# Slot tables of their own for the first, middle and last image and the tail, and another order of the opening, in an attention kernel

## The chip, the cores and the metric

One core of a Trainium2 chip runs the whole program. The metric is the device time of one execution in microseconds (us). The engines are TensorE (PE, with its weight loads as PEld), VectorE (DVE), ScalarE (ACT), GpSimd (POOL) and the DMA queues that SyncE (SP), POOL and ACT issue on.

## The reference

Eight images of 256 channels and 1024 positions go through three blocks, all in 32-bit floats.

```python
# block 0: group norm, 8-head attention (head width 32), projection, residual
qkv = einsum('oc,bcl->bol', w_qkv, group_norm(x)) + b_qkv
weight = softmax(einsum('bct,bcs->bts', q * scale, k * scale), axis=1)   # over the queries' axis
x = x + einsum('oc,bcl->bol', w_proj, einsum('bts,bcs->bct', weight, v)) + b_proj
t = to_tokens(x)
# block 1: layer norm, linear attention with elu(.)+1 features and rope, plus a 3-tap convolution
q, k = elu(ln(t) @ Wqk + bqk) + 1
t = t + rope(q) @ (rope(k)^T @ v) / (q . mean(k)) + conv3(ln(t))
# block 2: layer norm, Haar transform, interpolation, fc1, gelu, fc2, inverse Haar
t = t + idwt(fc2(gelu(fc1(interp(ll)))), lh, hl, hh)
```

## The kernel before

**Units.** The attention of an image is cut into 64 units: two groups of four heads, eight blocks of 128 keys, four heads. A unit s is: `scores` on PE (one 128x1024 product in the two-bank buffer `ps_s[s % 2]`), `maximum` on DVE (`negmax`, line 937), `exponentials` on ACT (`probs`, line 805). After each four units DVE inverts the sums (line 943, `rsums`), POOL scales the values by them (line 1213, `v_scaled`) and PE multiplies them with the probabilities (`weigh_values`, `ps_o`, line 585). q and k are each split in a high and a low part (`high_part` on ACT, line 839, `low_part` on DVE, line 982), and small DMAs stack these on the partitions of `q_st` and `k_st`: 16 of 128 KB for q and twice 16 of 64 KB for k, for each group of heads.

**Slots.** Each engine runs an in-order program, written out at build time: for each s from 0 to 63 first the unit's own instruction, then the steps that a hand-written table gives to slot s. PE runs one unit ahead: in slot s it issues `scores(s + 1)` first and then the steps. The steps are the rest of the work: `..._POST` tables hold blocks 1 and 2 of the image before (proj, x1T, lnT, qk, kT, kv, den, denT, out, uT, rT, ll, fc1, fc2, on POOL rsqrt, lepe, turn, pairs), `..._NEAR` tables the projections of this image's second group, `..._AHEAD` tables the next image's load, group norm (stats, moments, gn, squares, affine, apply) and first projections (pq0, pk0, pv0). Between engines only semaphores count, so that a slot number is an order on one engine and no moment. The same tables serve every image; the inverting, scaling and `weigh_values` stand in the loops at fixed places (s % 4 equal to 0, 1 and 2), as do the evictions of `ps_o` (slots 3, 4, 35, 36).

**Banks.** All steps of PE share two PSUM banks, `work[0]` and `work[1]`. `banks()` hands them out in turn over one middle image, and the prologue, the first and the last image take the same numbers, also where steps are missing and two tiles in a row get one bank. `claim` makes PE wait until the reader of the bank's tile before has read it. After the last image (`epilogue`) the tail's tables run with six banks.

**Opening.** SP loads the first image in two halves, then small constants, parameters and `w_qkv` (one semaphore, `early_in`), then the rest. PE waits for `early_in`, runs `warm_up(8)` (16 small products), the group means, `warm_up(18)`, then the tiles in the order pq0, pq0, pv0, pk0, pk0, pv0, and `scores(0, 0)`. SP stacks q of heads 0 and 1 and then k pieces, POOL q of heads 2 and 3 and then k pieces, ACT the k pieces of head 2.

## Time and profile before

| | us |
|---|---|
| median of 3 runs | 1459.22 |
| lowest and highest run | 1455.28, 1461.02 |
| the profiled execution | 1459.43 |
| its span, first to last instruction | 1457.6 |
| mean granted clock of TensorE | 0.944 |
| busy in the span: PE, DVE, ACT, POOL | 1228.9, 993.8, 878.9, 468.6 |

The page's fifth part groups the instructions by line; its second part cuts the span in 40 slices. The opening goes to about 38.6 us (the first `maximum`), each of the six middle images takes about 167 us, and the tail begins at 1352.4 us. Within a middle image a stretch is named by its times in image 2, which runs from 353.8 to 521.7 us.

### The profile page before, as it was taken

To read this page: it belongs to the slowest core of one execution; us is meant where nothing else is said; L and a number is where in the kernel's file an instruction comes from. 1 tells how busy PE (TensorE), PEld (TensorE's weight loads), DVE (VectorE), ACT (ScalarE), POOL (GpSimd) and SP (SyncE) were. 2 spreads that over 40 slices of the span, in tenths; PEclk is the share of its full clock that TensorE was granted. 3 is DMA by queue.
4 is the path that set the end of the run, shared out by engine and by line. 5 is a ranking of instruction groups with operands and counts; after the bars stand their busy time and mean duration, and the time that the engine had idled before them with its cause. 6 is when DMAs were issued, how large, how long until landed. Compare 5 with 4: busy or idle time off the path is not lost.

```text
span 1457.6 us, 21670 instructions
## 1 busy us (share of the span) xinstructions
PE 1228.9 (84%) x7724; PEld 621.8 (43%) x7724; DVE 993.8 (68%) x1607; ACT 878.9 (60%) x1457; POOL 468.6 (32%) x623
## 2 busy tenths in 40 slices
PE   5777799788987898889997899888988899979856
PEld 4423344444444444444444444444544444434343
DVE  2566587856878487766877568794878668784561
ACT  1556567665775667665774657656676657756412
POOL 2001016520364006530164203650065302650360
PEclk9798899999999999999999999999999999999977
DMA  7142315333242233432242232522243333310111
GB/s 250 31 117 62 80 32 106 71 85 98 62 108 60 55 83 86 89 87 78 66 80 78 63 99 61 114 55 56 81 92 84 87 81 71 76 50 15 35 24 44
DMA packets 51355, 111.27 MB, mean 76 GB/s; under 512 B 15505, under 2 KB 15761, under 8 KB 50993
## 3 DMA queue, kind: packets, MB, share of 16 engines
q1 hardware_dynamic: 48576, 100.85, 28.6%
q0 software_dynamic: 2480, 8.78, 2.0%
q8 instruction: 62, 1.02, 0.3%
q14 instruction: 45, 0.36, 0.1%
q10 hardware_dynamic: 192, 0.26, 0.1%
HBM read 21.75 MB, written 8.39 MB: 21 GB/s over the span
## 4 chain that ended last, share of the span: by engine, by line
PE 49%; DVE 24%; ACT 8%; issue 6%; SPq 5%; DMA 4%; POOL 2%; DVEq 0%; ACTq 0%; POOLq 0%
DVE negmax L937 11%; PE ps_s L570 11%; PE ps_o L585 11%; ACT probs L805 5%; PE work L716 4%; PE work L597 4%; PE work L721 4%; PE work L658 4%; PE work L644 4%; SPq L417 3%; PE work L609 3%; DVE ln_st L1002 3%; DVE tok L1013 3%; DMA xg<-in_x 2%; DVE t L1087 1%
## 5 line engine op out<-in xcount | busy, mean ns | idle before, releaser
L937 DVE TENSOR_REDUCE negmax<-ps_s 128x1 f32<-128x1024 f32 x512 | 619.7, 1214 | 294.1 <-PE ps_s L570 292.4
L805 ACT ACTIVATE probs<-ps_s,negmax 128x1024 f32<-128x1024 f32 x512 | 570.3, 1114 | 375.4 <-DVE negmax L937 369.9
L570 PE MATMUL ps_s<-q_st,k_st 128*128 128x512 f32 x1024 | 418.1, 494 | 118.0 <-ACT probs L805 106.5
L570 PEld LDWEIGHTS ps_s<-q_st,k_st 128*128 128x128 f32 x1024 | 171.0, 197 | 368.8 <-ACT probs L805 226.1
L585 PE MATMUL ps_o<-probs,v_scaled 128*32 128x512 f32 x2048 | 264.5, 637 | 5.1 <-POOL v_scaled L1213 5.1
L1213 POOL TENSOR_TENSOR v_scaled<-v_tok,rsums 128x128 f32<-128x128 f32 x128 | 51.3, 401 | 613.9 <-DVE rsums L943 613.9
L597 PE MATMUL work<-xg,w_qkv 128*128 128x512 f32 x256 | 122.9, 604 | 1.5 <-DVE t L1087 1.5
L585 PEld LDWEIGHTS ps_o<-probs,v_scaled 128*32 128x32 f32 x2048 | 56.1, 115 | 143.8 <-issue 131.4
L658 PE MATMUL work<-ln_ch,w_qk 128*128 128x512 f32 x232 | 110.6, 599 | 8.0 <-DVE k_ch L1113 8.0
L1272 POOL TENSOR_TENSOR x<-x,csum 128x1024 f32<-128x1024 f32 x45 | 106.7, 2370 | 3.2
L805 ACT ACTIVATION_READ_ACCUMULATOR probs<-ps_s,negmax 128x1 f32 x512 | 99.6, 195 | 0.0
L609 PE MATMUL work<-w_qkv,xg 128*128 128x128 f32 x512 | 67.8, 293 | 8.5 <-DVE lo L982 8.5
L839 ACT ACTIVATE hi<-work,par 128x512 fp32r<-128x512 f32 x62 | 42.3, 683 | 53.2 <-PE work L597 48.8
L716 PE MATMUL work<-band,w 128*128 128x512 f32 x118 | 63.6, 669 | 12.2 <-ACT band L877 12.2
L609 PEld LDWEIGHTS work<-w_qkv,xg 128*128 128x128 f32 x512 | 66.0, 207 | 14.1 <-DVE lo L982 12.0
L1244 POOL TENSOR_TENSOR ln_var<-ln_mv,con 128x2 f32<-128x2 f32 x64 | 13.1, 205 | 170.0 <-DVE ln_mv L1007 170.0
L597 PEld LDWEIGHTS work<-xg,w_qkv 128*128 128x128 f32 x256 | 47.1, 190 | 47.6 <-issue 35.0
L982 DVE SCALAR_TENSOR_TENSOR lo<-work,par,hi 128x512 fp32r<-128x512 f32 x62 | 46.4, 748 | 28.6 <-ACT hi L839 27.4
L658 PEld LDWEIGHTS work<-ln_ch,w_qk 128*128 128x128 f32 x232 | 42.7, 190 | 45.3 <-issue 28.6
L721 PE MATMUL work<-shared,w 128*128 128x512 f32 x128 | 60.3, 597 | 0.9 <-ACT shared L880 0.9
L644 PE MATMUL work<-att,w_proj 128*128 128x512 f32 x120 | 56.8, 597 | 0.0
L869 ACT ACTIVATE t<-work,par_elu 128x512 f32<-128x512 f32 x58 | 39.6, 683 | 26.0 <-PE work L658 26.0
(143 smaller groups left out, 1383.2 us busy)
## 6 DMA issues: line engine op xcount, KB each, us to landing
q_st<-hi SPq DMA_DIRECT2D x124, 128.0 KB, 2.4
q_st<-lo SPq DMA_DIRECT2D x124, 128.0 KB, 2.4
k_st<-hi SPq DMA_DIRECT2D x240, 64.0 KB, 2.0
k_st<-lo SPq DMA_DIRECT2D x240, 64.0 KB, 2.0
x<-in_x SPq DMA_DIRECT2D x8, 1024.0 KB, 5.0
out_x<-ln_ch SPq DMA_DIRECT2D x16, 512.0 KB, 2.8
xg<-in_x POOLq DMA_DIRECT2D x7, 1024.0 KB, 7.1
t<-shared SPq DMA_DIRECT2D x64, 64.0 KB, 2.3
```

The lines of the kernel that those rows point to most:

```text
L570: mm = pe.matmul(ps_s[s % 2][:, half * HALF:half * HALF + HALF], k_st[:, h, j * P:j * P + P], q_st[g][:, h, half * HALF:half * HALF + HALF ...
L585: mm = pe.matmul(ps_o[D * h:D * h + D, cols], v_scaled[:, j % 2, D * h:D * h + D], probs[:, j % 2, h, cols], start=(j == 0), stop=(j == NB ...
L597: mm = pe.matmul(bank(tile)[:, :], w_qkv[:, c, col:col + P], xg[:, c, half * HALF:half * HALF + HALF], start=(c == 0), stop=(c == NC - 1))
L609: mm = pe.matmul(bank(tile)[:, P * n:P * n + P], xg[:, c, P * nb:P * nb + P], w_qkv[:, c, col:col + P], start=(c == 0), stop=(c == NC - 1))
L644: mm = pe.matmul(ps[:, :], w_proj[:, g, P * c:P * c + P], att[:, g, half * HALF:half * HALF + HALF], start=(g == 0), stop=(g == 1))
L658: mm = pe.matmul(ps[:, :], w_qk[:, c, col:col + P], ln_ch[:, c, 1 + half * HALF:1 + half * HALF + HALF], start=(c == 0), stop=(c == NC - 1))
L716: pe.matmul(ps[:, :], w1[:, P * n:P * n + P], band[:, :], start=True, stop=True)\
L721: mm = pe.matmul(ps[:, :], w2[:, k, :], hid[:, k, :], start=(k == 0), stop=(k == 7))
L805: act.activation(probs[:, j % 2, h, :], ps_s[s % 2][:, :], ACT.Exp, bias=negmax[:, s % 4:s % 4 + 1], accum_out=sums[:, j % 2, h:h + 1]).th ...
L937: dve.tensor_reduce(negmax[:, s % 4:s % 4 + 1], ps_s[s % 2][:, :], AX_X, ALU.max, negate=True)\
L1213: pool.tensor_tensor(v_scaled[:, j % 2, :].rearrange("p (h d) -> p h d", h=HG), v_tok[g][:, j, :].rearrange("p (h d) -> p h d", h=HG), r.t ...
L1272: pool.tensor_tensor(x1[:, c, :], x1[:, c, :], lepe_product, ALU.add).then_inc(lepe_step, 1)
```

## The change

The shared tables go. Each engine gets a table for the first image, the middle ones, the last and the tail; the inverting ("invert"), scaling ("scale"), `weigh_values` ("values"), the evictions of `ps_o` ("copy") and the folding of a weight ("w1") are entries in them, at the slots that they had. Banks are handed out in turn over the whole program, image by image. Many steps stand in other slots. Of the tail's tables nearly all numbers are new; its order changes in places (kT tiles behind qk.6 and qk.7, uT.0 ahead of kv.1, `ll` ahead of the rT tiles). In the opening the constants and parameters are issued ahead of the image and have a semaphore of their own, k's first tile is made first, k of heads 0 to 2 is stacked first and then q head by head, rows 0 and 1 by SP and rows 2 and 3 by POOL; `warm_up(18)` becomes `warm_up(20)`, and PE waits for the scaled weights only behind it.

The middle images, slots of the steps that move (before, after):

```
PE    x1T.2 9,10  qk.6 27,28  den 32,31  denT 36,32  out.0 36,35  out.2 39,40  uT.0 40,39  uT.1 41,39
      uT.2 42,41  gn 38,39  rT.1 51,50  rT.3 52,51  fc1.1 49,48  pv0.1 60,56
ACT   x1T.1 9,10  x1T.2 10,11  qk.0 17,18  qk.3 23,22  qk.6 27,28  den 34,31  rT.3 52,51  ll 49,48
      apply.0 40,41  pq0 44 45,43 44
DVE   norm1.1 12,14  norm2.0 43,42  norm2.2 45,46  proj.2 8,9  x1T.2 11,12  qk.0 19,18  qk.1 20,19
      qk.3 24,23  qk.5 26,27  qk.6 28,29  kv.0 29,30  denT 36,33  out 38 38 40 42,37 39 41 41
      uT 41 42 43 43,40 40 42 43  up.0 63,61  stats 34 34 35 36,28 33 34 37  moments 37,38  gn 39,40
      pq0.0 45,44  pv0.1 61,63
POOL  rsqrt1 11 12 13 14,12 12 13 15  rsqrt2.0 38,39  kmean 29,32
      lepe 15 16 17 20 20 21 22 23 25 25 26 28,15 19 21 21 21 23 24 24 24 25 25 26
      turn 28 30 35 36 36 37,28 32 34 35 36 36  pairs.0 44,43  load 29,23  squares 37,38  affine 37,42
```

The core of the rest of the diff:

```diff
+FIRST_TILES = [("gn", 0), ("pk0", 0), ("pq0", 0), ("pq0", 1), ("pk0", 1), ("pv0", 0), ("pv0", 1)]
...
             def prologue():
+                for dst, src in ((con[:, 0:EARLY], consts[:, 0:EARLY]), (par[:, :], params)):
+                    sp.dma_start(dst, src).then_inc(const_in, DMA)
                 for c in range(NC):
                     sp.dma_start(xg[:, c, :], x_v[0][:, c]).then_inc(x_first[c], DMA)
-                for dst, src in ((con[:, 0:EARLY], consts[:, 0:EARLY]), (par[:, :], params),
-                                 (w_qkv[:, :, :], wqkv_t)):
-                    sp.dma_start(dst, src).then_inc(early_in, DMA)
+                sp.dma_start(w_qkv[:, :, :], wqkv_t).then_inc(early_in, DMA)
...
+                stack_first_k(sp, [(h, row) for h in range(3) for row in (0, 1)], first_stacked)
                 stack_first_q(sp, (0, 1), first_stacked)
-                stack_first_k(sp, ((0, 0), (0, 1), (1, 0), (1, 1), (3, 0), (3, 1)), first_stacked)
                 stack_k(sp, 0, 0, 1)
...
-        def stack_first_q(eng, heads, signals):
-            eng.wait_ge(lo_done, 2)
+        def stack_first_q(eng, rows, signals):
+            eng.wait_ge(lo_done, 1 + nth_split(0, ("pq0", 1)))
...
-                pe.wait_ge(early_in, EARLY_LOADS)
+                pe.wait_ge(const_in, CONST_LOADS)
                 warm_up(8)
-                pe.wait_ge(weights_ready, 1)
-                for tile in claimed(PE_AHEAD):
+                for tile in FIRST_TILES:
                     pre_tile("prologue", -1, tile)
                     if tile[0] == "gn":
-                        warm_up(18)
+                        warm_up(20)
+                        pe.wait_ge(weights_ready, 1)
                 scores(0, 0)
...
+                    for tile in due("PE", kind, s):
+                        step(kind, i, tile)
-                    if kind == "first":
-                        for tile in due(s, FOLD_AT):
-                            fold(kind, i, tile)
-                    if post:
-                        post_slot(kind, i, s)
-                    for tile in due(s, PE_NEAR, PE_AHEAD if ahead else {}):
-                        pre_tile(kind, i, tile)
-                    if s % HG == PV_AT:
...
-                stack_first_k(act, [(2, row) for row in range(4)], first_stacked)
+                stack_first_k(act, [(3, row) for row in range(4)], [first_stacked_act] * HG)
...
+                stack_first_k(pool, [(h, row) for h in range(3) for row in (2, 3)], first_stacked_pool)
                 stack_first_q(pool, (2, 3), first_stacked_pool)
-                stack_first_k(pool, ((0, 2), (0, 3), (1, 2), (1, 3), (3, 2), (3, 3)), first_stacked_pool)
```

## Rows read from the trace of the kernel before

**Rows 1.** The head of the page: the span.
```profile
span 1457.6 us, 21670 instructions
```

**Rows 2.** Windows by stage: length, busy us (instructions) per engine, clock, DMA share, GB/s.
```profile
core 0: us, PE busy (x) PEld busy (x) DVE busy (x) ACT busy (x) POOL busy (x), PEclk, DMA share, GB/s
38.60:185.20 146.60, 115.11 (x474) 48.16 (x473) 89.68 (x102) 84.29 (x140) 9.06 (x25) 0.83 0.29 72
...
353.80:521.70 167.90, 147.47 (x962) 75.07 (x961) 122.51 (x201) 109.47 (x182) 59.25 (x77) 0.98 0.33 79
...
688.80:863.30 174.50, 152.01 (x961) 76.20 (x960) 122.90 (x201) 109.47 (x182) 59.17 (x77) 0.95 0.32 76
...
1197.50:1352.40 154.90, 133.53 (x891) 65.42 (x894) 112.84 (x183) 102.74 (x173) 56.19 (x67) 0.96 0.24 58
1352.40:1457.60 105.20, 70.59 (x509) 41.67 (x508) 47.09 (x110) 29.75 (x46) 38.07 (x39) 0.79 0.14 36
```

**Rows 3.** Timeline of the opening to 18 us: start, length, engine, line, tiles, [idle before].
```profile
4.64 2.59 DVE L952 BATCH_NORM_STATS2 gn_stats<-xg 128x6 f32<-128x512 f32 x4 [4.64 <-DMA xg<-in_x]
...
9.39 0.50 DVE L1169 TENSOR_SCALAR w_qkv<-w_qkv 128x256 f32<-128x256 f32 x2 [1.83 <-DMA w_qkv<-in_wqkv_t]
...
9.41 3.78 PE L748 MATMUL ps_s<-con 128*128 128x128 f32 x16 [9.41 <-DMA w_qkv<-in_wqkv_t]
...
13.27 4.47 PE L748 MATMUL ps_s<-con 128*128 128x128 f32 x36
13.45 0.16 DVE L966 COPY gn_grp<-work 128x4 f32<-128x4 f32 x1 [3.34 <-PE work L615]
...
16.15 1.24 ACT L818 ACTIVATE xg<-xg,gn_sh,gn_a 128x1024 f32<-128x1024 f32 x1 [6.55 <-POOL gn_sh L1221]
...
17.57 3.60 PE L597 MATMUL work<-xg,w_qkv 128*128 128x512 f32 x8
```

**Rows 4.** Timeline of the opening from 21 to 45 us.
```profile
21.93 0.75 DVE L982 SCALAR_TENSOR_TENSOR lo<-work,par,hi 128x512 fp32r<-128x512 f32 x1 [0.96 <-ACT hi L839]
...
27.27 0.75 DVE L982 SCALAR_TENSOR_TENSOR att<-work,par,att 128x512 fp32r<-128x512 f32 x1 [0.96 <-ACT att L839]
...
30.80 4.89 SPq L433 DMA_DIRECT2D k_st<-att  x6
...
37.37 2.08 PE L570 MATMUL ps_s<-q_st,k_st 128*128 128x512 f32 x4 [8.96 <-DMA k_st<-att]
...
43.58 1.17 PE L570 MATMUL ps_s<-q_st,k_st 128*128 128x512 f32 x4
```

**Rows 5.** Windows: the stretch in which the first stacking lands.
```profile
27.00:38.00 11.00, 2.04 (x15) 1.75 (x14) 1.44 (x2) 0.23 (x1) 3.06 (x7) 0.67 0.91 233
```

**Rows 6.** Windows: two stretches of image 2.
```profile
432.40:475.70 43.30, 33.64 (x315) 20.10 (x312) 37.09 (x75) 24.42 (x40) 24.46 (x34) 0.96 0.33 91
480.00:506.00 26.00, 26.00 (x98) 11.20 (x96) 11.47 (x12) 15.85 (x26) 0.80 (x2) 1.00 0.02 3
```

**Rows 7.** Timeline of DVE, 432 to 476 us, image 2.
```profile
437.90 1.29 DVE L952 BATCH_NORM_STATS2 gn_stats<-xg 128x6 f32<-128x512 f32 x2 [1.87 <-DMA xg<-in_x]
...
453.16 0.68 DVE L1087 TENSOR_TENSOR t<-work,t 128x512 f32<-128x512 f32 x1
...
454.83 1.19 DVE L937 TENSOR_REDUCE negmax<-ps_s 128x1 f32<-128x1024 f32 x1
...
472.00 1.23 DVE L937 TENSOR_REDUCE negmax<-ps_s 128x1 f32<-128x1024 f32 x1 [2.05 <-PE ps_s L570]
```

**Rows 8.** Timeline of PE, 432 to 480 us, image 2.
```profile
441.67 0.73 PE L570 MATMUL ps_s<-q_st,k_st 128*128 128x512 f32 x2 [2.16 <-ACT probs L805]
...
467.97 3.53 PE L609 MATMUL work<-w_qkv,xg 128*128 128x128 f32 x16 [1.41 <-DVE lo L982]
```

**Rows 9.** Timeline of all engines, 500 to 522 us, the end of image 2.
```profile
506.84 0.75 DVE L982 SCALAR_TENSOR_TENSOR lo<-work,par,hi 128x512 fp32r<-128x512 f32 x1 [1.75 <-ACT hi L839]
...
520.38 1.19 PE L570 MATMUL ps_s<-q_st,k_st 128*128 128x512 f32 x4 [0.30 <-DMA k_st<-lo]
```

**Rows 10.** Timeline of image 2 near slot 19.
```profile
396.36 1.92 PE L585 MATMUL ps_o<-probs,v_scaled 128*32 128x512 f32 x16 [0.58 <-POOL v_scaled L1213]
```

More of the change, by code:

```diff
@@ L91 @@
[L91 to L97 removed]
+PE_FIRST = {
+    "w1": (25, 27), "pq1": (11, 12), "pv1": (0, 0), "pk1": (19, 20), "gn": (39,), "pq0": (43, 44),
+    "pk0": (49, 56), "pv0": (45, 56), "values": (6, 10, 14, 18, 22, 26, 30, 34, 38, 42, 46, 50, 54, 58, 62),
+}
@@ L546, in claim @@
             def claim(kind, i, tile):
-                before, earlier = tile_before(kind, tile)
+                before, earlier = tile_before(i, tile)
                 if before is None:
```

437 lines of the change are left out of this document (226 added, 211 removed), and 23 rows, old and new, of tables (DVE_LAST, DVE_POST, DVE_STEADY, DVE_TAIL).

## The prediction

> **What bounds the kernel now.** I read the windows by stage first, then the timelines of the stretches in which an engine idles. Rows 2 split the span: the first image takes 146.6 us, a middle one 167.9 us with PE busy for 147.5 and DVE for 122.5, the last 154.9, the tail 105.2. So 20.4 us in a middle image are not PE work: that is all that an order of steps can give there, if PE keeps its work. No single engine is the bound throughout. Three kinds of stretch are to be seen in image 2. From 480 to 506 us PE is busy for 26.00 of 26.00 us [rows 6]: it is the bound. From 432.4 to 475.7 us PE is busy for 33.6 of 43.3 us but DVE for 37.1 [rows 6]: DVE is the bound, and where it idles the time is lost: 1.87 us for the next image's load, 2.05 us for a score [rows 7]. From 507.6 us, where the low part of the last k tile ends (506.84 + 0.75), to 520.38 us the chain is 16 small DMAs and their landing, and the next image's first score waits 0.30 us for them [rows 9]: this chain of 12.8 us hangs from the low part alone. The opening is a fourth kind: until 37.37 us no score runs, and PE stands idle for 8.96 us before it, waiting for stacked k [rows 4].
>
> Image 4 (688.8 to 863.3) is 6.6 us longer than image 2 with the same instructions [rows 2]. It belongs to this execution; I leave it in the sum and give it as a spread.
>
> **The opening, first half.** Before, PE begins to warm up at 9.41, when `w_qkv` is there; the group means follow its 16 products, and the copy of them is at 13.45, though the statistics had ended at 7.23 [rows 3]. After, constants and parameters are issued first, so PE warms up while the image lands. The image is issued two transfers later. The gap between two issues of SP stands in no row here; from the second load on the bytes ahead are the same, so I take the statistics 0 to 1.3 us later (the upper end is half their own 2.59), 1.0 taken. They end at 8.2, and with means and squares the product of the means is at 9.2. DVE still has to scale the weights behind `w_qkv` (9.39 + 0.50 [rows 3], and three small ones): the copy is at 10.1. From the copy to the apply it took 16.15 - 13.45 = 2.70, and the apply 1.24 [rows 3]: the normed image is there at 14.0, where it was at 17.4.
>
> But `warm_up(20)` is 40 products, begun at 9.5 us. The first 16 took 3.78 us, 0.236 each, the 36 behind them 4.47 us, 0.124 each [rows 3]: the two levels of the clock. At the fast one they end at 14.5, at the slow one at 18.9. PE's first warming products lie before a hole of about 1 us, so neither is excluded. I take the fast level from the first quarter on: PE's first projection at S = 15.5, before at 17.57 [rows 3]. The gain is 2.1, bounds -1.3 and 3.1.
>
> The Trainium skill ("TensorE: Matmul & The Clock Gate", Part 1) says that the fast clock is the answer to activity and goes with idleness, and that its windows run free of the program. By that rule the split warming could go the slow way in one execution and the fast way in the next. It is the third rival.
>
> **The opening, second half.** Before, the low part of q was there at 22.68 and that of k at 28.02; SP issued q of heads 0 and 1 first and its last six k pieces at 30.80 to 35.69; heads 0 and 1 both began at 37.37, heads 2 and 3 at 43.58, behind PE's pv1 tiles [rows 4]. That is 19.8 and 26.0 us behind the first projection. The stacking itself is bound by transfer: from 27 to 38 us the DMA engines are busy for 0.91 and move 233 GB/s [rows 5]. Its 16 x 128 KB and 16 x 64 KB are 3.1 MB, 13.5 us at that rate. After, nothing of this volume goes away; what changes is when it starts and what a head waits for. k's first tile is ready 3.5 us behind S (a tile of four products is 3.60 / 2 = 1.8 [rows 3]; high part, low part and their waits, 1.7, a little above twice 0.75). Twelve k pieces then take 0.8 MB, 3.4 us at the rate of rows 5, about 2.5 us to landing. q's second tile comes 1.8 us behind q's first; its low part is there at S + 6.8. A head's q is 0.5 MB, 2.3 us. So head 0 is complete at about S + 11, head 1 at S + 13, head 2 at S + 15.5, head 3 at S + 18. PE has its seven tiles done at S + 11 too. Then score 0, score 1, and the two pv1 tiles (43.58 - 39.4 = 4.2, [rows 4]) until S + 18, scores 2 and 3 at S + 18 to S + 19.5, that is 33.5 to 35, where they were at 43.58. The gain behind score 3 is 8.5 to 10, the whole opening 10.0 with the first half's part in it; bounds 6 and 12.
>
> **The first image.** Its order hardly changes; the banks now alternate, the statistics move into slots where DVE idles in any case (busy for 89.7 of 146.6 [rows 2]). 0, with 2.5 either way for the clock, which is 0.83 there [rows 2] and follows PE's gaps.
>
> **Middle images, to slot 31.** POOL's convolution steps (lepe) gave way late to a scaling, and PE waited 0.58 us for `v_scaled` [rows 10]. The new table has one step between those two scalings and seven between the next two, with the load behind them. That block is long, but the next values on PE are two slots off. I take 0.3 (PE loses part again where qk.6 goes one slot back), bounds -0.7 and 1.0.
>
> **Middle images, slots 32 to 48.** This is the term that counts. The load leaves POOL's order at 23 rather than 29, so some 20 us earlier than the statistics need it: DVE's 1.87 and, in the units' ring, PE's 2.16 [rows 7, 8] go (one event, counted once). One statistic (1.29 / 2 = 0.65 [rows 7]) leaves the stretch. denT is made early and fills PE's time. The pv0 tile took 3.53 us for 16 products behind a gap of 1.41 [rows 8], at a clock of which rows 6 show 0.96 for the whole stretch; DVE's 2.05 is that tile's shadow [rows 7]. Against it stands a new wait: `gn` on PE (slot 39) now takes uT.0's bank, so PE waits there for DVE's slot 40, and `scores(41)` is queued behind it; DVE then does two uT tiles of 454.83 - 453.16 = 1.67 us each [rows 7] before it copies `gn`. The ceiling is DVE's own work: 43.3 - 37.1 + 0.65 = 6.9 us. The floor is 0: every idle moment replaced by another. I take 1.87 + 2.05 gone, a quarter of the remaining 2.3 of idleness gone, 1.0 given to the new wait: 3.5.
>
> **Middle images, slots 49 to 63.** PE is the bound to 506 us [rows 6] and its work is the same, so the 3.5 pass through. pv0.1 moves from slot 60 into PE's wait in slot 57; that gives nothing, since the chain of 12.8 us [rows 9] sets the end. So a middle image gives 3.8; six of them 22.8.
>
> **Last image and tail.** The last image has no load, statistics or gn; 1.0, bounds 0 and 3. The tail's order moves a few waits; POOL's turning steps stay one chain. 0, 3 either way.
>
> **Sum.** 10.0 + 22.8 + 1.0 = 33.8 from the profiled execution's 1459.4 (its span is 1457.6 [rows 1]), which is the median of the runs to 0.2 us: 1426.
>
> **The rivals.** (1) Waits replaced. DVE and PE only trade waits in slots 32 to 48, and a middle image gives 1.0: 1459.4 - 9 - 6 = 1444. For it: ACT, DVE and PE wait for each other in a ring of two score buffers, so that a gap closed at one place opens at the next. Against it: the 1.87 us are a wait for a transfer, which no reordering of the ring brings back. 0.25. (2) All idleness of DVE in the stretch goes but a fifth: 5.5 + 0.3 per image, 12 in the opening: 1459.4 - 34.8 - 12 - 1 = 1412. For it: DVE has no gap but these in rows 6. 0.12. (3) The clock is slow in `warm_up(20)`: S = 18.9 rather than 15.5, all else as forecast: 1429. 0.13. (4) Slower. The new claim of `gn`: its copy comes behind two uT tiles, then POOL's affine chain (behind rsqrt2.1) and the apply on ACT, in front of the exponentials and of pq0, whose low part starts everything up to the next image. By my order pq0 still begins about 1 us earlier than before. It decides from the point where the copy comes over 1 us later than that; at two uT tiles more, 3.3 us, each image loses 2.3 beyond what it gained: 1459.4 - 10 + 13.8 = 1463. 0.04. (5) The tables change but the engines' order in time doesn't, since slots are no moments; the opening alone acts: 1449. 0.06. The forecast has 0.40.
>
> **How the numbers follow.** 1426 is the likeliest case's. Its own terms reach from 1418 to 1436. The range 1411 to 1446 takes in rivals 1, 2 and 3 and leaves out 4 and 5, some 2 in 10 with the edges; the 6.6 us of image 4, which may be there or not, are within it. About 0.5% (7.3 us) is what a measurement of this kernel can tell from no change, so faster begins below 1452: the forecast, 1, 2, 3 and nearly all of 5, less a little for unforeseen waits, 0.91. Same 0.05, slower 0.04.
>
> **What would show it.** In the changed kernel's profile: PE's first L597 near 15.5, the first score near 27 and scores 2 and 3 by 35, with heads one after the other; the copy of the means at 10. No idle time of DVE before L952 in any middle image. A middle image of about 164 us, with the stretch from slot 32 to 48 down to about 40 us, and PE still full from fc1 to fc2. It is wrong if PE shows gaps of over 1 us before L615 with a release by DVE t, if ACT's L818 starts later in the image than before, or if the middle images come out above 167.

## The result: 1397.1 us, nearly twice the forecast gain

The changed kernel takes 1397.1 us (median; 1393.4 to 1398.3), the kernel before on the same chip 1458.6; the ratio is 0.958 with a 95% interval of 0.955 to 0.960. The forecast was 1426 us, its range 1411 to 1446: 61.5 us were gained where 33.8 had been worked out. The profiled execution took 1396.6 us, so the trace stands for the median to 0.6 us. Three single runs of experiments that were far longer than the others of their kernel (1912.9, 6427.5 and 1647.0 us) are left out of the times below. Its span, from the head of its page:

```profile
span 1394.8 us, 21679 instructions
```

The windows by stage (columns as in [rows 2]; first image, image 2, last image):

```profile
30.60:175.70 145.10, 112.51 (x475) 48.35 (x476) 89.83 (x102) 84.51 (x140) 9.03 (x25) 0.85 0.33 81
336.30:496.10 159.80, 146.27 (x959) 73.78 (x959) 122.33 (x200) 109.34 (x182) 59.09 (x77) 0.99 0.35 83
...
1138.00:1289.10 151.10, 135.80 (x893) 66.24 (x896) 113.52 (x184) 103.11 (x173) 56.16 (x67) 0.96 0.24 56
```

Against [rows 2], PE's busy time in image 2 is nearly the same (146.3 for 147.5), the image is 8.1 us shorter, and 13.5 us are left in which PE is idle, of 20.4. Cut at the first `maximum` of each image (slots by the order of the 512 `maximum` instructions), the two traces differ like this, in us:

| | before | after | gain | forecast |
|---|---|---|---|---|
| start of image 1 (opening and first image) | 185.2 | 175.7 | 9.5 | 10.0 |
| six middle images, slots 0 to 31, mean of one | 77.5 | 75.0 | 2.5 | 0.3 |
| slots 32 to 48 | 45.0 | 40.5 | 4.5 | 3.5 |
| slots 49 to 63 | 46.2 | 44.9 | 1.3 | 0 |
| last image | 155.0 | 151.2 | 3.8 | 1.0 |
| tail | 105.2 | 105.8 | -0.6 | 0 |

Opening and slots 32 to 48 came out near the forecast. The excess lies in slots 0 to 31, in slots 49 to 63 and in the last image, 24 us together; slots 32 to 48 add 1.0 in each of six images.

The first line stands for one execution. The changed kernel and the thirteen variants below that keep its opening have the same first image, and it ends between 175.1 and 181.4 us in their traces (mean 177.7); with the opening of before it ends between 185.2 and 186.0. So 8 us is the better figure for this line, and 175.7 is one of the luckier executions.

In the changed kernel's code the lines are others: `scores` is L608 (was 570), `weigh_values` L623 (585), `maximum` L970 (937), `exponentials` L841 (805), the projections L635 and L647 (597, 609), qk on PE L696 (658), kT L704, its DVE part L1146 (1113), gn L653, out L736, ll L749, fc1 L754, the copy of ll's band on ACT L913 (877), the turning steps on POOL L474 to L480.

The opening in the timeline of the changed kernel (PE's two warm-ups, copy of the means, first projection, the four first scores):

```profile
3.45 3.78 PE L794 MATMUL ps_s<-con 128*128 128x128 f32 x16 [3.45 <-DMA par<-in_params]
...
9.78 6.34 PE L794 MATMUL ps_s<-con 128*128 128x128 f32 x40
9.96 0.16 DVE L999 COPY gn_grp<-work 128x4 f32<-128x4 f32 x1
...
15.96 7.21 PE L635 MATMUL work<-xg,w_qkv 128*128 128x512 f32 x16
...
29.78 0.73 PE L608 MATMUL ps_s<-q_st,k_st 128*128 128x512 f32 x2 [2.93 <-DMA q_st<-hi]
33.83 1.22 PE L608 MATMUL ps_s<-q_st,k_st 128*128 128x512 f32 x2 [3.31 <-DMA q_st<-hi]
34.85 5.41 PE L647 MATMUL work<-w_qkv,xg 128*128 128x128 f32 x32
40.02 1.17 PE L608 MATMUL ps_s<-q_st,k_st 128*128 128x512 f32 x4
```

It answers to [rows 3, 4]: the means are copied at 9.96 (forecast 10.1), the first projection starts at 15.96 (15.5), the first score at 29.78 (27), scores 2 and 3 at 40.02 (33.5 to 35).

### The profile page after: what moved, and what is told of

It reads as the page before. It is cut to its first block, busy times and chain, and to the rows that moved or that the text cites. A ratio compares the mean times of both kernels' runs of the same rounds, so it can differ in the third digit from the quotient of the medians.

```text
span 1394.8 us, 21679 instructions
## 1 busy us (share of the span) xinstructions
PE 1227.2 (88%) x7728; PEld 621.5 (45%) x7728; DVE 992.1 (71%) x1607; ACT 879.8 (63%) x1457; POOL 467.0 (33%) x623
## 4 chain that ended last, share of the span: by engine, by line
PE 53%; DVE 28%; ACT 9%; issue 6%; SPq 1%; DMA 1%; POOL 0%; DVEq 0%; POOLq 0%; ACTq 0%
DVE negmax L970 13%; PE ps_s L608 12%; PE ps_o L623 12%; ACT probs L841 7%; PE work L696 6%; PE work L635 4%; PE work L759 4%; PE work L754 3%; DVE tok L1046 3%; PE work L682 3%; DVE ln_st L1035 3%; PE work L647 2%; PE work L736 2%; DVE t L1120 1%; DVE lo L1015 1%
## 5 line engine op out<-in xcount | busy, mean ns | idle before, releaser
L970 DVE TENSOR_REDUCE negmax<-ps_s 128x1 f32<-128x1024 f32 x512 | 620.0, 1215 | 243.2 <-PE ps_s L608 241.6
L841 ACT ACTIVATE probs<-ps_s,negmax 128x1024 f32<-128x1024 f32 x512 | 570.4, 1114 | 321.4 <-DVE negmax L970 316.3
L608 PE MATMUL ps_s<-q_st,k_st 128*128 128x512 f32 x1024 | 408.7, 485 | 78.0 <-ACT probs L841 67.9
L608 PEld LDWEIGHTS ps_s<-q_st,k_st 128*128 128x128 f32 x1024 | 168.8, 195 | 328.3 <-ACT probs L841 198.1
L623 PE MATMUL ps_o<-probs,v_scaled 128*32 128x512 f32 x2048 | 267.6, 643 | 0.5 <-POOL v_scaled L1240 0.5
L635 PE MATMUL work<-xg,w_qkv 128*128 128x512 f32 x256 | 122.2, 601 | 2.8 <-ACT xg L854 2.8
L623 PEld LDWEIGHTS ps_o<-probs,v_scaled 128*32 128x32 f32 x2048 | 55.9, 113 | 133.7 <-issue 132.1
L696 PE MATMUL work<-ln_ch,w_qk 128*128 128x512 f32 x236 | 113.0, 601 | 2.4 <-DVE k_ch L1146 2.3
L841 ACT ACTIVATION_READ_ACCUMULATOR probs<-ps_s,negmax 128x1 f32 x512 | 99.5, 194 | 0.0
L635 PEld LDWEIGHTS work<-xg,w_qkv 128*128 128x128 f32 x256 | 47.9, 191 | 49.4 <-issue 39.8
L754 PE MATMUL work<-band,w 128*128 128x512 f32 x118 | 57.1, 615 | 10.0 <-ACT band L913 5.9
L647 PEld LDWEIGHTS work<-w_qkv,xg 128*128 128x128 f32 x512 | 62.5, 196 | 5.5 <-issue 3.3
L647 PE MATMUL work<-w_qkv,xg 128*128 128x128 f32 x512 | 62.6, 280 | 0.0
L1015 DVE SCALAR_TENSOR_TENSOR lo<-work,par,hi 128x512 fp32r<-128x512 f32 x62 | 46.2, 745 | 22.6 <-ACT hi L875 22.6
L696 PEld LDWEIGHTS work<-ln_ch,w_qk 128*128 128x128 f32 x236 | 43.1, 190 | 40.6 <-issue 29.1
L1296 POOL TENSOR_SCALAR csum<-ln_ch,par 128x1024 f32<-128x1024 f32 x45 | 54.0, 1199 | 0.0
```

What stands on the lines that cost most here:

```text
L608: mm = pe.matmul(ps_s[s % 2][:, half * HALF:half * HALF + HALF], k_st[:, h, j * P:j * P + P], q_st[g][:, h, half * HALF:half * HALF + HALF ...
L623: mm = pe.matmul(ps_o[D * h:D * h + D, cols], v_scaled[:, j % 2, D * h:D * h + D], probs[:, j % 2, h, cols], start=(j == 0), stop=(j == NB ...
L635: mm = pe.matmul(bank(tile)[:, :], w_qkv[:, c, col:col + P], xg[:, c, half * HALF:half * HALF + HALF], start=(c == 0), stop=(c == NC - 1))
L647: mm = pe.matmul(bank(tile)[:, P * n:P * n + P], xg[:, c, P * nb:P * nb + P], w_qkv[:, c, col:col + P], start=(c == 0), stop=(c == NC - 1))
L696: mm = pe.matmul(ps[:, :], w_qk[:, c, col:col + P], ln_ch[:, c, 1 + half * HALF:1 + half * HALF + HALF], start=(c == 0), stop=(c == NC - 1))
L754: pe.matmul(ps[:, :], w1[:, P * n:P * n + P], band[:, :], start=True, stop=True)\
```

## The experiments

Unless it is said otherwise, an experiment is the changed kernel with one part put back or moved; two are the kernel before with one part of the change. The step tables are meant; what isn't named stays. "More" and "less" compare with the 1397.1 us above. The changed kernel was timed only then; the kernel before came out at 1457.0 to 1460.3 us in the rounds of the experiments, and one variant, timed in two rounds, at 1400.3 and 1406.4. So a difference of under some 6 us between two kernels below is not firm.

### One part put back at a time

**The opening** of before (order of the loads, starts, warm-ups, tile order, stacking).

> The changed kernel (1397.1 us) with the opening of before: image issued ahead of the constants, PE, ACT and POOL waiting for the weights too, 18 warming calls, tiles in the order q, q, v, k, k, v, q of heads 0 and 1 stacked by SP and of heads 2 and 3 by POOL ahead of the k pieces. All slot tables stay new. Theory A (the opening's gain is what the fourth maximum shows, 45.5 us before and 41.9 us after): about 3.6 us slower, 1400.7, and the first image's new table keeps the other 5.9 us that the start of image 1 has gained (185.2 to 175.7). Theory B (as forecast, the opening is worth 10 and the first table nothing): 1407.

Measured 1405.6 (1403.7 to 1409.1), 8.5 more, near what theory B had. The first score is at 37.43, and image 1 starts at 185.7 us, as in the kernel before (185.2): the first image's new table gives nothing by itself.

**Load and statistics.**

```diff
-"load": (23,)                +"load": (29,)
-"stats": (28, 33, 34, 37)    +"stats": (34, 34, 35, 36)
```

> The changed kernel with POOL's load of the next image back at slot 29 and DVE's four statistics back at slots 34, 34, 35, 36. Theory A (the wait for the load cost every middle image its own length, as forecast): DVE idles 1.6 to 2.5 us in front of the statistics again and six images lose 2 to 2.7 us each, 12 to 16 us in all: 1409 to 1413. Theory B (with the other slots redrawn there is room for the wait, or the wait was shadowed by PE): under 4 us, below 1401.

Measured 1410.6 (1408.0 to 1412.4), 13.5 more, as theory A had it; by which mechanism is told below, and it isn't the one expected.

**qk and kv.**

```diff
 PE  -"qk": (17, 18, 21, 22, 24, 25, 28, 29)  +(17, 18, 21, 22, 24, 25, 27, 29)
 ACT -"qk": (18, 18, 21, 22, 24, 25, 28, 30)  +(17, 18, 21, 23, 24, 25, 27, 30)
 DVE -"qk": (18, 19, 22, 23, 25, 27, 29, 31)  +(19, 20, 22, 24, 25, 26, 28, 31)
 DVE -"kv": (30, 35)                          +(29, 35)
```

> The changed kernel with the steps of qk (PE, ACT, DVE) and DVE's kv back in their old slots, 17 to 31, middle images and last. Theory A (a q or k tile read one slot sooner frees its bank before PE gets there, which the forecast had not counted): 2 to 3 us for each of seven images, 1411 to 1418, with PE's gap of about 1.1 us at the fifth qk tile back. Theory B (as forecast, 0.3 us per image): 1397 to 1399.

Measured 1413.0 (1412.2 to 1414.7), 15.9 more: the largest part, where the forecast had 1.8.

**Slots 31 to 47** (den, denT, out, uT, norm2, gn, moments, turn, pairs and what goes with them).

> The changed kernel with den, denT, out, uT, norm2, moments, gn, squares, affine, apply, pq0's eviction, kmean, turn, rsqrt2 and pairs back in their old slots (31 to 47); load and statistics stay early. Theory A (the redrawn order there is worth about 2 us per image beside the load): seven images, 12 to 16 us slower, 1409 to 1413. Theory B (the early load does it all and the order itself gives nothing): within 3 us of 1397.

Measured 1409.5 (1403.8 to 1413.9), 12.4 more: theory A.

**POOL's lepe.**

> The kernel after with POOL's slots of the local term (lepe) as in the kernel before, in the steady and last tables, nothing else. The single parts so far undone sum to 50.4 of 61.5 us; the rest, 11, lies in the parts not yet undone and in the 7 us of image 4. Theory A (POOL's queue is a bound in slots 20 to 28: lepe ahead of the turning steps makes the kv products late): 6 x 1 us and more, 1403 or above. Theory B (lepe fills POOL's idle time and only its order changes): within 2 us of the changed kernel, 1395.5 to 1399.

Measured 1398.8 (1395.0 to 1400.8), 1.6 more, no difference that can be told: theory B.

**The late steps** (rT, fc1, ll, pv0.1, up).

> The kernel after with rT, fc1, ll, the second value tile pv0.1 and the upsampled rows (up) in the slots of before. In the median middle image, slots 49 to 63 are 1.0 us shorter after the change, mostly at slots 58 and 59. Theory A (pv0.1 in PE's wait for the DMA chain at slot 56 to 57 is what takes that 1.0 away, since PE doesn't fall to its slow clock before the products of the next image): 6 x 1.0 and 1 for rT, 1404 (1402 to 1406). Theory B (the chain of transfers sets the end, as the prediction had it, and pv0.1's place gives nothing): 1397 to 1399.

Measured 1406.3 (1401.3 to 1409.4), 9.2 more. By its size this spoke for theory A; the separation below shows that pv0.1 isn't the cause.

The six parts sum to 61.1 of 61.5 us. That they meet so well is in part luck: the 13.5 us of the load hold some 8 us of a collision that neither kernel has (below), so that without it the parts give 53, and 8 us of the gain are in none of them. The tail's tables and the new order of the banks were not put back by themselves. Whether the parts are independent was asked with **three put back together** (qk and kv, load, slots 31 to 47):

> The kernel after with three parts undone together that were undone singly before: the qk and kv slots, the early load with its statistics, and the order of slots 31 to 47. Singly they cost 15.9, 13.5 and 12.4 us, 41.8 together, against the changed kernel's 1397.1. Theory A (separate gaps on one bound chain, each worth its own time wherever it stands): the costs add, 1438.9 (1434 to 1443). Theory B (the three open the same slack: one new wait hides part of another, so that each single undo counts a shared loss twice, once it is there the next costs less): about 30 us, 1427. Theory C (they support each other, and what is left of the change doesn't work without them): beyond 46 us, over 1443.

Measured 1435.2 (1429.9 to 1436.7), 38.1 more against 41.8 by the sum, nearer to theory A. But in this kernel `kmean` stands ahead of the load again and the collision isn't there: POOL's turning step waits for no copy. Against the single costs without the collision, 34, the three together cost 4 more. Neither difference is beyond the spread, so the run speaks against theories B and C and says no more.

### The qk ring: eviction slots or PE's slots?

```diff
 ACT -"qk": (18, 18, 21, 22, 24, 25, 28, 30)  +(18, 18, 21, 23, 24, 25, 28, 30)
 DVE -"qk": (18, 19, 22, 23, 25, 27, 29, 31)  +(19, 20, 22, 24, 25, 26, 29, 30)
```

> The kernel after with the evictions of qk tiles 3 to 5 on ACT (slots 23, 24, 25 for 22, 24, 25) and on DVE (24, 25, 26 for 23, 25, 27, and tile 6 and 7 at 29, 30 for 29, 31) as in the kernel before, PE's slots as changed. The whole qk part cost 15.9 us, 2.5 in slots 24 to 31 of each middle image. Theory A (ring of two work buffers: PE waits for an eviction one slot late, ACT for PE, DVE for ACT; the evictions' slots alone make the gap): 6 x 1.5 to 2.5, 1406 to 1412. Theory B (PE's slots of the tiles decide): within 3 us of the kernel after, to 1400.

Measured 1421.5 (1420.7 to 1429.2), 24 more: theory A in kind, worse in size. DVE's eviction of tile 7 went to slot 30 here, where neither kernel has it (31 in both), and so ahead of DVE's copy of kv in the same slot; PE then waits for that copy, in image 2:

```profile
416.04 0.66 PE L704 MATMUL work<-con,k_ch 128*128 128x128 f32 x4 [2.37 <-DVE kv_c L1078]
```

So this kernel shows where the wait of the ring comes from, not what it costs. What evictions one slot late do is seen in the timelines (idle time before an instruction, and its releaser, in brackets). The kernel before, image 2:

```profile
409.90 1.23 DVE L937 TENSOR_REDUCE negmax<-ps_s 128x1 f32<-128x1024 f32 x1 [1.38 <-PE ps_s L570]
...
411.91 1.99 PE L658 MATMUL work<-ln_ch,w_qk 128*128 128x512 f32 x4 [1.14 <-DVE k_ch L1113]
...
413.99 0.69 ACT L869 ACTIVATE t<-work,par_elu 128x512 f32<-128x512 f32 x1 [1.57 <-PE work L658]
```

The changed kernel, the same slots:

```profile
391.73 1.23 DVE L970 TENSOR_REDUCE negmax<-ps_s 128x1 f32<-128x1024 f32 x1
...
392.51 1.88 PE L696 MATMUL work<-ln_ch,w_qk 128*128 128x512 f32 x4
...
394.48 0.69 ACT L905 ACTIVATE t<-work,par_elu 128x512 f32<-128x512 f32 x1 [0.23 <-PE work L696]
```

The kernel with the evictions alone put back:

```profile
395.37 1.22 DVE L970 TENSOR_REDUCE negmax<-ps_s 128x1 f32<-128x1024 f32 x1 [1.37 <-PE ps_s L608]
...
397.38 1.99 PE L696 MATMUL work<-ln_ch,w_qk 128*128 128x512 f32 x4 [1.14 <-DVE k_ch L1146]
```

DVE waits 1.38 for a score, PE 1.14 for DVE's reading of a qk tile, ACT 1.57 for PE: one loop, three waits. The slots of ACT and DVE make it: with PE's as changed and theirs back (ACT tile 3; DVE tiles 0, 1, 3 and 5), the same 1.37 and 1.14 return. Which of these tiles does it wasn't taken apart. The windows of slots 24 to 31 in image 3 say what it is worth. Before:

```profile
577.60:599.00 21.40, 19.08 (x210) 9.45 (x208) 17.01 (x29) 15.41 (x26) 11.18 (x13) 1.00 0.47 91
```

After, and behind it slots 32 to 39, 40 to 48 and 49 to 55:

```profile
551.50:570.90 19.40, 18.49 (x208) 9.07 (x206) 16.86 (x27) 14.35 (x26) 14.39 (x15) 1.00 0.66 150
...
570.90:587.00 16.10, 14.12 (x208) 7.61 (x207) 14.72 (x26) 10.96 (x19) 11.33 (x9) 1.00 0.24 55
...
587.00:611.80 24.80, 21.79 (x121) 13.31 (x119) 23.19 (x51) 13.77 (x22) 13.35 (x25) 0.93 0.31 83
611.80:636.10 24.30, 22.87 (x97) 10.58 (x97) 9.34 (x10) 19.89 (x31) 0.95 (x3) 1.00 0.21 47
```

PE is busy for 18.5 of 19.4 us there now: it had 2.3 idle, it has 0.9. Then the other way round, **qk and kv alone in the kernel before**, with nothing else changed:

> The kernel before, with the qk and kv slots of after on PE, ACT and DVE and nothing else. Taken out of the changed kernel they cost 15.9 us, 2 to 2.5 us in slots 24 to 31 of each image. Theory A (a wait in a ring of PE, ACT and DVE, removed by taking qk tile 3 out of the buffer a slot sooner; what stands elsewhere in the image plays no part): slots 24 to 31 fall from 21.35 to about 19.4, 1459 - 12 to 16: 1443 to 1447. Theory B (POOL's turning steps and kmean in their old slots take the place of the wait at once): under 6 us, 1453 or above.

Measured 1438.3 (1437.4 to 1440.4), 17 to 19 less than the kernel before in those rounds (ratio 0.988, interval 0.984 to 0.993). Its window of the same slots:

```profile
572.10:591.50 19.40, 18.64 (x209) 9.26 (x207) 16.26 (x26) 14.37 (x26) 11.15 (x13) 1.00 0.50 96
```

It is the changed kernel's 19.4 in the old surroundings: theory A, and more than it had. The ring itself gives 1.9 us in each of six middle images and the last, 13.6 us. The rest stands in slots 32 to 48 (45.0 before, 43.7 here), where the clock is slow in slots 40 to 48 of one middle image rather than four, and a stop of PE in image 4, told below, is 0.92 us rather than 4.19; that part may be this execution's. With qk put back in the changed kernel slots 24 to 31 take 21.9 us in all six images. So four lines of slot numbers are worth 14 to 16 us by themselves.

### The late steps: the value tile or the fold?

**rT, fc1 and ll put back**, pv0.1 as changed:

```diff
 PE  -"rT": (47, 50, 51, 51)  +(47, 51, 51, 52)
 PE  -"fc1": (48, 48, 49, 49, 49, 49, 49, 49)  +(48, 49, 49, 49, 49, 49, 49, 49)
 ACT -"rT": (47, 51, 51, 51), "ll": (48,)  +(47, 51, 51, 52), "ll": (49,)
```

> The kernel after with the slots of before for rT, fc1 and ll alone (pv0.1 and up as changed). All of the late part together cost 9.2 us; in its trace slots 49 to 55 were 26.36 us in most middle images against 24.34, with a gap of 2.04 us on PE ahead of fc1 (now 0.84 and 0.60), and slots 56 to 59 up to 13.5 against 11.89. Theory A (the wait before fc1 is the cause of the first: it is a loss of 0.6 by itself and drops the clock for the products behind it): most of the 9.2, 1404 to 1410. Theory B (pv0.1 out of slot 56 is the cause of both): 1396 to 1400.

Measured 1408.3 (1403.5 to 1413.7), 11.2 more. **pv0.1 and up put back**, the rest as changed:

> The kernel after with the slots of before for the second value tile (PE 60, DVE 61) and the upsampled rows (63, 63) alone, rT, fc1 and ll as changed. Theory A (the wait before fc1 makes the loss in slots 49 to 55): slots 49 to 55 stay at 24.3; slots 56 to 59 become 13 in some images, slots 60 to 63 become 7.95 rather than 8.69, and the first twelve 24.9 rather than 25.4: 1395 to 1400. Theory B (pv0.1 in slot 56 holds the clock and gives the 9.2): 1403 to 1408.

Measured 1395.2 (1390.5 to 1399.0), 1.9 less than the changed kernel, within the spread. Theory A both times: the fold carries all, the value tile nothing. Image 3 of the kernel with the fold put back, first ACT, then PE:

```profile
623.35 1.11 ACT L841 ACTIVATE probs<-ps_s,negmax 128x1024 f32<-128x1024 f32 x1
...
624.46 0.58 ACT L913 COPY band<-work 128x512 f32<-128x512 f32 x1
```

```profile
625.17 1.67 PE L754 MATMUL work<-band,w 128*128 128x512 f32 x2 [2.03 <-ACT band L913]
625.85 1.84 PE L608 MATMUL ps_s<-q_st,k_st 128*128 128x512 f32 x2
627.49 7.48 PE L754 MATMUL work<-band,w 128*128 128x512 f32 x14
```

The changed kernel, first ACT, then PE:

```profile
612.96 0.57 ACT L913 COPY band<-work 128x512 f32<-128x512 f32 x1
613.43 1.13 ACT L841 ACTIVATE probs<-ps_s,negmax 128x1024 f32<-128x1024 f32 x1
```

```profile
613.68 1.96 PE L754 MATMUL work<-band,w 128*128 128x512 f32 x4 [0.84 <-ACT band L913]
615.07 1.03 PE L608 MATMUL ps_s<-q_st,k_st 128*128 128x512 f32 x2
616.70 5.79 PE L754 MATMUL work<-band,w 128*128 128x512 f32 x12 [0.60 <-ACT shared L916]
```

With `ll` in ACT's slot 48 the copy goes ahead of an exponential of 1.1 us, and PE waits 0.84 and then 0.60 us rather than once 2.03. These 0.6 us are the smaller part. Behind the wait of 2.03 the next score takes 1.84 us rather than 1.03: the granted clock is 0.50 there, TensorE at 1.2 GHz and not at 2.4. Slots 49 to 55 take 26.6 us (mean of six), against 24.3. The windows of these slots and of the slow stretch in the same image (the changed kernel's, above, has 1.00):

```profile
622.10:648.40 26.30, 24.27 (x97) 11.22 (x97) 9.34 (x10) 19.95 (x31) 0.95 (x3) 0.94 0.19 43
...
625.60:629.00 3.40, 3.40 (x6) 1.68 (x5) 1.22 (x1) 1.42 (x2) 0.00 (x0) 0.50 0.52 117
```

The Trainium skill ("TensorE: Matmul & The Clock Gate", Part 1) says that activity releases the throttle and idleness brings it back. In direction these rows agree: in these slots the slow clock followed a wait of 2.03 us in all six images and one of 1.74 (before) in three. Behind one of 0.84 it is in none of the changed kernel's images, but in two with pv0.1 put back and in three with the load in slot 32 (slots 49 to 55 at 25.1 to 25.2 us). So a shorter wait makes it rarer and doesn't exclude it.

**The same three steps alone in the kernel before:**

> The kernel before, with three steps in the slots of after and nothing else: rT (slots 47, 50, 51, 51 on PE, 47, 51, 51, 51 on ACT), ll on ACT in 48, and the second tile of fc1 in slot 48 on PE. Taken out of the changed kernel they cost 11.2 us: PE then waits 2.03 us for ACT's band ahead of fc1, and the matmuls behind run at the slow clock. In the kernel before that wait is 1.74 us, and slots 49 to 55 take 24.7 us in three images and 26.3 in the others. Theory A (the wait and the clock behind it are a loss by themselves, whatever the other parts are): slots 49 to 55 become 24.3, 0.4 to 2 us per image, the median 1459 - 7 to 11: 1448 to 1452. Theory B (it gives only in the changed kernel's surroundings): 1456 to 1461.

Measured 1452.9 (1451.0 to 1458.2), ratio 0.997 (0.996 to 0.999): 4.3 us. The mechanism is the same (slots 49 to 55 fall from a mean of 25.5 to 24.6, PE's wait from 1.74 to 0.82 and 0.59), but less than theory A had: slots 56 to 59 rise from 12.8 to 13.1, they are long (13.0 to 13.5) in five of six images where they were in four. In the changed kernel they take 11.9 in all six; with pv0.1 put back, 12.8 in the mean. So pv0.1 in slot 56 does gain there, and gives it back in slots 60 to 63 (8.7 for 7.9) and 0 to 11.

### The load: traffic or collision?

In the kernel with the load in slot 29, POOL's and PE's timelines show in image 3:

```profile
572.72 0.79 POOL L424 DMA_DIRECT2D xg<-in_x  x1
...
581.21 2.00 POOL L474 TENSOR_TENSOR att<-att,con 128x1024 f32<-128x1024 f32 x1 [4.65 <-DMA att<-shared]
```

```profile
592.43 1.13 PE L736 MATMUL work<-kv_c,shared 128*128 128x128 f32 x8 [2.32 <-issue]
```

SP's last copy `att<-shared` was issued at the same moment as the load of 1 MB, and POOL's turning step waited for it 4.65 us, to 1.0 us behind the load's last packet (580.2). PE's wait is put down to "issue", but it ends where POOL's last turning step does (589.99 + 2.34 = 592.33). To separate this from traffic as such, a **spare transfer** of the same size in slot 29 for which nobody waits, with the load in 23:

> The kernel after, its load where it is (slot 23), and a second transfer of the same image (1 MB, same queue, from the input to a spare tensor in the chip's memory) issued by POOL in slot 29 of each middle image, for which nobody waits. With the load itself moved to slot 29 a kernel took 13.5 us more, and in its trace PE's long waits at L736 end with POOL's turning steps, which had waited for the copies att<-shared; DVE's wait for the load was not there. Theory A (it is the traffic of the load in slots 29 to 34 that makes the copies for the turning steps late): the spare transfer costs as much with nobody waiting for it, 1397 + 8 to 14, some 1408. Theory B (it is the statistics' place or DVE's wait for the load that costs, not the traffic): 1397 to 1400.

> The same kernel as in the run with the spare transfer in slot 29, again, because its profile of then can't be read (granted clock 0.582); 3.2 to 4.9 us more than the kernel after were measured. Theory A (collision with the copies att<-shared): POOL idle 2 us and more at L474 for the DMA att<-shared in some of the middle images, where the kernel after has none, and slots 32 to 39 longer in just these. Theory B (traffic plays no part): no such idle time, and slots 32 to 39 as in the kernel after, 15.8 to 16.1 us.

Measured 1400.3 in the first (1397.6 to 1403.8) and 1406.4 (1404.0 to 1414.0) in the second: 3 and 9 more, though nobody waits for it. The second's trace has what theory A asked for: POOL waits 1.9 to 5.1 us for `att<-shared` in five images, with slots 32 to 39 at 17.3 to 20.1 us, and not in the sixth, with 16.0. Last, the **load in slot 32**, behind the turning step that waits:

```diff
-"load": (23,)               +"load": (32,)
-"stats": (28, 33, 34, 37)   +"stats": (36, 36, 37, 37)
```

> The kernel after with the load in slot 32 of the middle images, in POOL's queue right behind the turning step that waits for the copies att<-shared, and the statistics in slots 36, 36, 37, 37. With the load in slot 29 (13.5 us more), SP's last of eight copies att<-shared was issued together with the load (572.77 and 572.72 in one image) and landed only 8 us later, for which POOL's turning step idled 4.65 us and behind it PE's tiles at L736. Here the load is issued later still, but with no copy of that kind under way. Theory A (the load costs by its collision with these copies alone): near the kernel after, 1397 to 1402. Theory B (a load of 1 MB in slots 29 to 36 costs wherever it is, by its traffic beside the k_st transfers or by the late statistics): 1407 to 1415.

Measured 1402.8 (1398.2 to 1404.5), 5.7 more, just beyond theory A's range. What ended the waits of POOL before its steps on `att`, summed over the span (us, times): load in 29, then the spare transfer:

```profile
  DMA att<-shared: 15.3, 5
```

```profile
  DMA att<-shared: 14.9, 5
```

In the kernel before, after, and with the load in 32 there is no such wait. In the last the order is:

```profile
575.21 2.00 POOL L474 TENSOR_TENSOR att<-att,con 128x1024 f32<-128x1024 f32 x1
577.15 0.79 POOL L424 DMA_DIRECT2D xg<-in_x  x1
```

So more than half of the 13.5 us is a collision that my experiment made: in the kernel before the load is in slot 29 too, but `kmean` stands ahead of it in POOL's queue and waits for k, so that the load is issued 4.8 to 6.7 us behind SP's last copy in the six middle images, and no turning step waits. In the changed order nothing holds it back, and it meets them. Putting one step back isn't the same as the step's share of the gain. What is left for a late load without the collision is 5.7, at the edge of what can be told, with slots 32 to 39 at 17.3 us rather than 15.9 (means of six). Some 15 us of POOL's waiting went with 13.5 and 9.3 us of time. The load alone moved to slot 23 in the kernel before wasn't run, so what the early load gives of the 61.5 us isn't shown.

### Three more

**gn ahead of uT** (PE 39 to 38, DVE 40 to 39): the forecast's rival 4 had seen a wait there.

> The kernel after with PE's product of the group means (gn) one slot earlier, ahead of the first two uT tiles, and its copy on DVE one slot earlier, as in the kernel before; nothing else. In the changed kernel PE waits 1.10 and 0.69 us there in a middle image, for DVE's uT additions. Theory A (those two waits are a loss that the place of gn makes): they go, and some 1 to 1.8 us per image with a gn come back, 1386 to 1391, faster than the kernel after. Theory B (the ring of buffers closes on PE in any case, and the means are then behind POOL's squares, which PE would wait for): no gain, 1396 to 1400; with the means late, slower, up to 1405.

Measured 1401.9 (1401.3 to 1402.8), 4.8 more: no gain, theory B. In the changed kernel the waits are there:

```profile
429.64 0.39 PE L653 MATMUL work<-gn_mom,con 128*128 128x4 f32 x2 [1.10 <-DVE t L1120]
...
431.29 1.16 PE L736 MATMUL work<-kv_c,shared 128*128 128x128 f32 x8 [0.69 <-DVE t L1120]
```

With gn first they change their name and DVE loses more:

```profile
592.23 0.36 PE L653 MATMUL work<-gn_mom,con 128*128 128x4 f32 x2 [1.04 <-POOL gn_mom L1248]
...
595.14 1.23 DVE L970 TENSOR_REDUCE negmax<-ps_s 128x1 f32<-128x1024 f32 x1 [1.85 <-PE ps_s L608]
```

**Both value tiles late** (pv0 on PE 56 and 60), to keep the clock in slots 60 to 63:

> The kernel after with PE's value tiles pv0 in slots 56 and 60 (rather than 45 and 56) and their copies on DVE in 58 and 62 (rather than 47 and 63). In the changed kernel the products ps_o of slot 62 run 3.21 us at the slow clock, since PE has nothing in slots 60 and 61, and slots 60 to 63 take 8.69 us against 7.95 before. Theory A (a tile in slot 56 keeps the clock for slots 57 to 59, one in slot 60 for slots 61 to 63; slots 40 to 49 get a tile less on PE and DVE, which are both full there): 0.7 + 0.5 + 0.3 to 1.5 us less in each of six images, 1397 - 9 to 16, 1385, faster than the kernel after. Theory B (the values come too late for the next image's first products, and slots 60 to 64 have DVE as the bound): no gain, 1396 to 1405.

Measured 1395.7 (1392.1 to 1399.8), 1.4 less, no difference that can be told: slots 60 to 63 fall from 8.7 to 8.2 and 40 to 48 from 24.6 to 23.6, slots 49 to 55 rise from 24.3 to 25.0. None of the variants is faster than the changed kernel beyond the spread.

**The order of tiles and stacking put back, the early starts kept:**

> The kernel after with the order of the first tiles and of the stacking transfers of before (queries first; heads side by side over the queues), but with the new order of the loads and the earlier start of PE, ACT and POOL. The whole opening costs 8.5 us. By the prediction S, the start of PE, moved by about 5 us and the order of keys and heads gives the rest. Theory A (the start gives it, the order of the transfers little): 1397 + 0 to 3. Theory B (the order decides, since the stacking transfers queue behind each other): 1397 + 4 to 8.

Measured 1400.8 (1398.1 to 1404.9), 3.6 more, between the two theories. Its opening, in the longest of the four runs:

```profile
10.02 7.55 PE L794 MATMUL ps_s<-con 128*128 128x128 f32 x40
...
17.41 1.45 PE L635 MATMUL work<-xg,w_qkv 128*128 128x512 f32 x3
```

```profile
37.22 2.07 PE L608 MATMUL ps_s<-q_st,k_st 128*128 128x512 f32 x4 [8.90 <-DMA k_st<-att]
```

The 40 products took 7.55 us here and 6.34 above, so the projection began where it had before the change [rows 3], and the first score is at 37.22, as there [rows 4]. Of the 7.4 us by which this score is later than in the changed kernel, the projection's start is 1.45 and the order the rest, 6. In this run image 1 starts at 184.7 us, 7 later than the mean of the kernels with the changed opening; in the median of the times only 3.6 us arrive. How the 8.5 us of the opening divide stays open.

## Why the prediction was wrong in size

**The opening: the total right, by luck in its second half.** 10.0 forecast, 9.5 in the two traces, 8.5 by putting it back. The first half met its numbers to 0.5 us. The warm-up was neither fast (5.0 us for 40) nor slow (9.4): 6.34, and 7.55 in another kernel, so rival 3 is real as a spread of about 1.5 us. The second half failed. Score 0 came at 29.78 (27 forecast), head 1 waited another 3.31 us for its q, the pv1 tiles took 5.4 us rather than 4.2, and scores 2 and 3 came at 40.0 and not by 35: behind score 3 the gain was 3.6 us, where 8.5 to 10 had been worked out. The first image, forecast at 0, then gained the rest up to its end, 5.9 us in this pair of traces. It isn't its table (the run with the opening put back has that too), and why the early heads' start is worth more by then stays open.

**Right in size: slots 32 to 48.** 3.5 forecast, 4.5 in the mean, of which 0.7 is image 4's stop of 4.2 us (below). DVE's wait for the load (1.6 to 2.5 us in all six images before) is gone. Rival 4's wait for gn's bank is there, 1.10 and 0.69 us, which is also what the prediction had named as a sign that it is wrong (a gap of over 1 us before gn, released by DVE t); the run with gn first shows that moving gn doesn't win it back. Slots 32 to 39 gave 4.0 of the 4.5 and 40 to 48 only 0.5. The other half of the forecast, DVE's 2.05 us at slot 47, had been read from image 2 for all: it stood in four of six images. It is gone, but in five images DVE now waits 1.2 to 1.4 us at slot 41, and these ran slots 40 to 48 in 24.8 us at a clock of 0.93, as above, and one in 23.5.

**The step that failed: "Middle images, to slot 31".** It has 0.3 per image; the traces show 2.5, and both runs on the part alone 16 to 19 us over the kernel, 14 to 16 of them in slots 24 to 31. I had costed POOL's scaling and the tile qk.6, and put at nothing the evictions of the qk tiles, which moved one slot each (tile 3 on ACT, tiles 0, 1 and 3 on DVE a slot sooner). The waits of 1.38, 1.14 and 1.57 us stood in the trace of before at slots 23 to 25 of every middle image; I had looked for idle time only where DVE was called the bound. The prediction's kinds of stretch (PE full, DVE nearly full, the transfer chain, the opening) leave out slots 0 to 31, and with them a stretch in which neither engine is full: PE 19.1, DVE 17.0 of 21.4 us.

**The second: "Middle images, slots 49 to 63".** 0 forecast, 1.3 measured, 9 to 11 us over the kernel. "PE is the bound to 506 us and its work is the same" rested on a window from 480 us [rows 6]. PE's wait of 1.74 us for the band copy ended at 478.85 us, just ahead of it. And it rested on image 2, the luckier kind: slots 49 to 55 took 24.7 us there and in two other middle images, but 26.2 to 26.4 in the remaining three. A bound engine's work isn't constant when its clock isn't. The other half of that step, pv0.1 worth nothing, was right (-1.9 us measured).

**The last image.** 1.0 forecast, 3.8 measured: it has the qk ring and the fold too, 2 us each.

**The rivals.** The waits weren't replaced (1), and the idle time removed was more than DVE's in one stretch (2). The order of the parts by size was wrong: opening, load and slots 31 to 47, on which the sum rested, gave 8.5, 5.7 (without the collision) and 12.4 us, qk and the fold, which it had at 1.8 and 0, 15.9 and 11.2.

**Image 4.** The prediction took its 6.6 us as belonging to that one execution. The traces speak against that. PE's timeline there in the kernel before:

```profile
769.32 1.41 PE L674 MATMUL work<-tok,shared 128*32 128x32 f32 x127
774.92 0.26 PE L674 MATMUL work<-tok,shared 128*32 128x32 f32 x1 [4.19 <-issue]
```

PE stops within a tile of 128 matmuls, where no instruction waits for another engine, for 4.19 us. The DMA view from 772 to 774 us (packets, MB, share):

```profile
q1 hardware_dynamic: 236, 0.31, 66.1%
q8 instruction: 1, 0.02, 3.8%
```

One packet of the instruction queue starts at 772.3, behind the load, whose packets filled the queues to 771.5 (from 770 to 772 they held 55% of the DMA engines). In the kernel before with rT and fc1 changed, another program, the stop is behind the same 127th matmul; in the changed kernel with the opening of before it is behind the 122nd, though the load was issued 28 us ahead of the stop's end there (9 us in the kernel before):

```profile
773.77 0.22 PE L674 MATMUL work<-tok,shared 128*32 128x32 f32 x1 [3.66 <-issue]
```

```profile
749.20 0.26 PE L712 MATMUL work<-tok,shared 128*32 128x32 f32 x6 [1.76 <-issue]
```

So it repeats, and it doesn't need the load. In the traces of this case, the one of the 1912.9 us run left aside, there are 20 such stops of 0.7 to 4.2 us within a tile of 128 of these matmuls, one of them in the changed kernel (0.93 us, image 2), and in each PE goes on 2.3 to 2.8 us behind the start of a 16 KB packet of the instruction queue. The two longest, 4.19 and 3.66 us, are those with the load just ahead. That PE waits there for its own code, and longer behind a load, is the reading that fits; no run took it apart, so it isn't shown.

## What to carry to other kernels

Before costing a change of order, list the idle time of every engine in every stretch, above all of those in which none is full: a wait of 1.1 to 1.6 us on each of three engines around two buffers is one loop, and evictions that are one slot late close it in every image. A wait of PE can have a second price in TensorE's clock: of the 2.3 us that slots 49 to 55 lost, 0.6 were waiting. Before a wait read in one image is multiplied by six, look for it in the others: DVE's 2.05 us stood in four of six, the long slots 49 to 55 in three. And a step put back into a changed schedule can meet work that it never met before, so that its cost isn't its share of the gain: try the step in the old kernel as well.

## What was not expected of the hardware

- A copy of SP that was issued with a 1 MB load on POOL's queue held its reader up until the load was through: POOL's step started 1.0 to 1.5 us behind the load's last packet in five of six images, and in the sixth didn't wait. With the spare transfer it started 0.6 to 1.1 us behind in five. The Trainium skill ("DMA: Bandwidth & Descriptors", "Issuing engines are not separate DMA queues") says that transfers of all issuing engines run on the same 16 DMA engines and interleave. Sharing is what is seen, and interleaving only over longer stretches: in image 3 of the kernel with the load in slot 29, from 575 to 577 us, the DMA view has packets of the load's queue alone, while copies for `k_st` and the last ones `att<-shared` had been issued by SP (its queue is q1) and hadn't landed.

```profile
q0 software_dynamic: 176, 0.72, 93.1%
```

- TensorE's clock makes one stretch with the same instructions two lengths: slots 40 to 48 take 23.5 or 24.8 us in the changed kernel, PE busy for 20.4 or 21.8. Kernels that are the same there differ in how many of their six images get which: one of six is the short one in the changed kernel, all six with the qk evictions alone put back.
- An idle label "issue" had two causes: a step of POOL (592.43, above) and what looks like missing code (774.92).
